# New hand-written orders of the instructions on all engines in a perceiver block (one core)

## What is computed

```python
# part 1: decoder, 4 layers, 16 heads of 16 features
for l in range(4):
    h  = rmsnorm(x, n1[l]);  q, k, v = split(h @ Wqkv[l].T + bqkv[l])
    q, k = rope(q), rope(k)
    x += softmax(q @ k.T / 4 + causal) @ v @ Wo[l].T + bo[l]
    qc = rmsnorm(x, n2[l]) @ Wq_c[l].T
    kc, vc = split(memory @ Wkv_c[l].T)      # keys j with itok-128 < j <= itok
    x += softmax(qc @ kc.T / 4 + lookback) @ vc @ Wo_c[l].T
    h3 = rmsnorm(x, n3[l])
    x += silu(h3 @ Wg[l].T) * (h3 @ Wu[l].T) @ Wd[l].T      # 1024 wide
# part 2: each token attends with sigmoids to its 16 predecessors, then layernorm, gamma, beta
# part 3: gated FFN of width 1024: weights rounded to -1, 0, 1 times mean |w|, activations to 8 bits
```

## Time and profile before

| | us |
|---|---|
| three runs | 622.4, 620.0, 622.28 |
| median | 622.28 |
| the profiled execution | 619.67 |
| its span in the trace | 617.9 |
| mean granted clock of TensorE in it | 0.991 |

### The profile page before, as it was taken

How to read it: one execution, slowest core, us unless ns; L and a number is a source line. 1 busy time by engine, 2 the same in 40 slices (tenths; PEclk the granted TensorE clock), 3 DMA queues, 4 the chain that set the end, 5 groups by cost and what they waited for, 6 DMA issues and landing times.

```text
span 617.9 us, 13676 instructions
## 1 busy us (share of the span) xinstructions
PE 564.1 (91%) x5806; PEld 421.8 (68%) x5806; DVE 353.5 (57%) x680; ACT 279.5 (45%) x490; POOL 117.7 (19%) x124
## 2 busy tenths in 40 slices
PE   4989998999999899999998989999898989999855
PEld 1666655988767566988766658987666558897523
DVE  5896445466564454674554455574554364752787
ACT  0254444633355336433544446342554547445523
POOL 4252100012323100020612000122312001252110
PEclk9999999999999999999999999999999999999969
DMA  8800020010500200201400200204000200000001
GB/s 334 345 2 25 12 69 2 5 65 1 205 2 4 102 1 3 68 1 27 180 1 36 70 2 2 69 1 189 16 2 1 71 0 2 0 1 2 2 1 39
DMA packets 4676, 30.29 MB, mean 49 GB/s; under 512 B 1153, under 2 KB 1665, under 8 KB 2818
## 3 DMA queue, kind: packets, MB, share of 16 engines
q1 hardware_dynamic: 4610, 29.35, 12.5%
HBM read 28.82 MB, written 0.52 MB: 47 GB/s over the span
## 4 chain that ended last, share of the span: by engine, by line
PE 77%; DVE 10%; ACT 8%; issue 3%; POOL 1%; DMA 1%; SPq 0%; DVEq 0%; POOLq 0%
PE psD L326 18%; PE QD L621 12%; PE psD L634 9%; PE QD L408 6%; PE QD L443 4%; ACT PTR L1253 3%; PE psD L320 3%; PE QD L436 3%; PE QD L394 3%; DVE AQ L1803 3%; PE psD L463 2%; PE QD L431 2%; PE psD L359 2%; PE psD L484 2%; PE psD L470 2%
## 5 line engine op out<-in xcount | busy, mean ns | idle before, releaser
L1253 ACT ACTIVATE PTR<-QD 128x2048 f32<-128x2048 f32 x40 | 75.1, 1878 | 41.8 <-PE QD L443 21.5
L326 PE MATMUL psD<-WAB,hT 128*128 128x256 f32 (+1 forms) x216 | 70.1, 465 | 2.2 <-DVE hT L1744 2.2
L2492 POOL TENSOR_TENSOR rstd<-ms,mhalf 128x2 f32<-128x2 f32 x26 | 19.9, 764 | 271.8 <-DVE ms L1729 270.6
L1803 DVE TENSOR_REDUCE AQ<-QD 128x8 f32<-128x2048 f32 (+1 forms) x24 | 55.0, 2290 | 27.0 <-PE QD L408 27.0
L621 PE MATMUL QD<-HH,WFH 128*128 128x256 f32 x224 | 67.4, 301 | 0.4 <-DVE WFL L1903 0.4
L1903 DVE TENSOR_TENSOR WFL<-WC,WFH 128x512 fp32r<-128x512 f32 x64 | 48.0, 755 | 32.2 <-ACT WFH L1297 32.1
L621 PE MATMUL QD<-HL,WFH 128*128 128x256 f32 x224 | 63.3, 283 | 0.0
L621 PE MATMUL QD<-HH,WFL 128*128 128x256 f32 x224 | 63.3, 283 | 0.0
L1800 DVE TENSOR_REDUCE AQ<-QD 128x16 f32<-128x2048 f32 x16 | 36.7, 2293 | 39.9 <-PE QD L408 39.9
L634 PE MATMUL psD<-WC,HID 128*128 128x256 f32 x256 | 58.2, 380 | 0.0
L326 PEld LDWEIGHTS psD<-WAB,hT 128*128 128x128 f32 x216 | 39.7, 195 | 21.0 <-issue 14.2
(11 more groups left out here) (172 smaller groups left out, 1021.2 us busy)
## 6 DMA issues: line engine op xcount, KB each, us to landing
WC<-in_wc SPq DMA_DIRECT2D x4, 3072.0 KB, 10.9
WAB<-in_wa SPq DMA_DIRECT2D x4, 1024.0 KB, 4.9
WAB<-in_wb SPq DMA_DIRECT2D x4, 1024.0 KB, 4.7
WF<-in_wf SPq DMA_DIRECT2D x1, 3072.0 KB, 22.8
bias<-in_bias SPq DMA_DIRECT2D x4, 512.0 KB, 3.4
WAB<-in_wt SPq DMA_DIRECT2D x1, 1024.0 KB, 6.0
X<-in_x SPq DMA_DIRECT2D x2, 256.0 KB, 2.8
out_x<-X SPq DMA_DIRECT2D x4, 128.0 KB, 2.4
```

The source lines that it names most:

```text
L326: mm = pe.matmul(bank(l, use)[:, col:col + n], lhs(k), rhs(k), start=(k == 0), stop=(k == KT - 1))
L1253: nc.scalar.activation(PTR[:, r % 2, :], QD[:, :], ACT.Exp, scale=SCALE).then_inc(t_exp, 1)
L1803: v = dve.tensor_reduce(QKR[b][:, t, 0, h, MAXROW].rearrange("p (s r) -> p r s", r=SG_H), QD[:, :].rearrange("p (r s n) -> p r s n", r=4, ...
```

## The change

On TensorE, ScalarE, VectorE and GpSimd the calls of the helpers stand in another order. The calls are the same in kind and number on each engine; no helper is changed, and SP's queue is not. The cuts between prologue, `layer` and the last layer are put elsewhere: on TensorE `layer(l)` now begins with `down(l - 1, 0, ...)` and ends with `gate_up(l, 0, 7)`; on ScalarE it begins with `exp(l, 6)` and ends with `squares(l + 1, 1, 1)`; on VectorE it ends with `residual(l + 1, 0, "wo0")`; on GpSimd it begins with `causal(l, 3)`. The number of blocks is read, and the branch taken, after `pv(0, 1)` on TensorE (before: after `cross_qT(0, 1, 1)`), after `query_max_strips(0, 1)` on ScalarE, after `sines(0, 1, 1)` on GpSimd, and after `cross_q(0, 0)` on VectorE.

TensorE, one layer (layers 1 to 3; in layer 0 alike in its second half). The first block is the order before, the second the new one, from `values(l, 0)` to `cross_qT(l, 0, 1)`:

```diff
-values(l, 0)            maxima_T(l, 1)          norm_T(l, 0, 1)
-scores(l, 2)            queries_keys(l, 1, 0)   pv(l, 0)
-scores_T(l, 1)          maxima_T(l, 2)          outputs_T(l, 0)
-queries_keys(l, 1, 1)   scores_T(l, 2)          rotated_T(l, 1, 0, 1)
-pv(l, 1)                rotated_T(l, 1, 0, 0)   values(l, 1)
-scores(l, 3)            rotated_T(l, 1, 1, 0)   outputs_T(l, 1)        pv(l, 2)
+values(l, 0)            norm_T(l, 0, 1)
+scores(l, 2)            maxima_T(l, 1)          queries_keys(l, 1, 0)  pv(l, 0)
+scores_T(l, 1)          queries_keys(l, 1, 1)   maxima_T(l, 2)
+rotated_T(l, 1, 0, 1)   rotated_T(l, 1, 0, 0)   scores_T(l, 2)
+outputs_T(l, 0)         pv(l, 1)
+scores(l, 3)            rotated_T(l, 1, 1, 0)   outputs_T(l, 1)        pv(l, 2)
...
 out_proj(l, 0, "wo0", Wo, "oT0")
+maxima_T(l, 4)
 scores(l, 5)
-maxima_T(l, 4)
 cross_kT(l, 0)
-pv(l, 3)
+values(l, 1)
 scores_T(l, 4)
 norm_T(l, 1, 0)
 maxima_T(l, 5)
-outputs_T(l, 3)
+pv(l, 3)
 cross_q(l, 0)
 scores_T(l, 5)
+cross_qT(l, 0, 0)
+outputs_T(l, 3)
 pv(l, 4)
-cross_qT(l, 0, 0)
 cross_qT(l, 0, 1)
```

TensorE, all layers, rounds 8 and 9, and the tail:

```diff
 maxima_T(l, 9)
 norm_T(l, 2, 0)
+pv(l, 8)
 scores_T(l, 9)
-pv(l, 8)
 gate_up(l, 0, 0)
-gate_up(l, 0, 1)
 outputs_T(l, 8)
 pv(l, 9)
+gate_up(l, 0, 1)
+outputs_T(l, 9)
 gate_up(l, 0, 2)
 gate_up(l, 0, 3)
 gate_up(l, 0, 4)
-outputs_T(l, 9)
 gate_up(l, 0, 5)
...
 rounded_T(0)
+window_pv(1, 1)
 quantised_gate_up(0, 0)
+out_proj(NL, 1, "mwo1", Wt[:, 3, :, :], "pw1")
 quantised_gate_up(0, 1)
-window_pv(1, 1)
 quantised_gate_up(1, 0)
-out_proj(NL, 1, "mwo1", Wt[:, 3, :, :], "pw1")
-hidden_T(0)
 quantised_gate_up(1, 1)
 rounded_T(1)
 quantised_gate_up(2, 0)
 quantised_gate_up(2, 1)
+hidden_T(0)
```

ScalarE, last layer (the rounds 1 to 5 of the last layer now stand at the end of `layer`, without sums between them):

```diff
 sum_abs(0)
 sum_abs(1)
 sum_abs(2)
-self_strips(NL - 1, 1, 0, 1)
-strip_outputs(NL - 1, 1)
...
-exp(NL - 1, 3)
 sum_abs(3)
-squares(NL - 1, 1, 0)
...
-exp(NL - 1, 4)
 sum_abs(4)
-exp(NL - 1, 5)
 sum_abs(5)
-query_strips(NL - 1, 0, 0)
...
-squares(NL - 1, 1, 1)
 exp(NL - 1, 6)
 sum_abs(6)
 query_max_strips(NL - 1, 7)
 exp(NL - 1, 7)
 sum_abs(7)
...
 exp(NL - 1, 8)
 sum_abs(8)
 query_max_strips(NL - 1, 9)
+strip_outputs(NL - 1, 8)
 exp(NL - 1, 9)
 sum_abs(9)
 sum_abs(10)
 sum_abs(11)
-strip_outputs(NL - 1, 8)
 split_high(NL - 1, 3)
+strip_outputs(NL - 1, 9)
 silu_table()
```

VectorE, prologue, and its tail:

```diff
 normalise(0, 0, 0)
+small_constants()
+weigh_T(0, 0, 0)
 layernorm_stats(1, 1, X0)
-weigh_T(0, 0, 0)
...
 maxima(0, 0)
+biased_v(0, 0)
+maxima(0, 1)
 biased_qk(0, 1, 0)
 cosines(0, 1, 0)
-maxima(0, 1)
-biased_v(0, 0)
+blocks_to_go()
+maxima(0, 2)
 add_sines(0, 1, 0)
-maxima(0, 2)
 biased_qk(0, 1, 1)
 cosines(0, 1, 1)
-blocks_to_go()
+masks()
+add_sines(0, 1, 1)
 biased_v(0, 1)
-add_sines(0, 1, 1)
-masks()
 divide(0, 0)
...
 quantised_hidden(0, 0)
-quantised_hidden(0, 1)
-hidden_scales(0)
-quantised_hidden(1, 0)
 window_sum(1)
 layernorm_stats(5, 1, X)
 window_gamma(1)
 window_residual(1)
+quantised_hidden(0, 1)
 layernorm_stats(7, 1, X0)
-round_hidden(0)
+hidden_scales(0)
 layernorm_apply(7, 1, X0, hs, done)
+quantised_hidden(1, 0)
...
 round_hidden(3)
+hidden_T(2)
 output(0)
-hidden_T(2)
```

More of the change, by code:

```diff
@@ L835, in layer @@
                 gate_up(l, 0, 7)
[L836 to L878, removed]
             pe.wait_ge(c_ld, 16)
@@ L1000, in rest @@
-                rotated_T(1, 0, 0, 0)
-                gate_up(0, 1, 7)
-                pe.wait_ge(consts_set, 1)
-                scores(1, 0)
-                rotated_T(1, 0, 1, 0)
-                down(0, 1, range(0, 4))
-                scores(1, 1)
-                down(0, 1, range(4, FT))
-                maxima_T(1, 0)
-                rotated_T(1, 0, 1, 1)
-                scores_T(1, 0)
-                values(1, 0)
-                maxima_T(1, 1)
-                norm_T(1, 0, 1)
-                scores(1, 2)
@@ L1031, in rest @@
                     layer(l, further)
+                down(NL - 2, 0, range(0, 4))
+                norm_T(NL - 2, 2, 1)
+                down(NL - 2, 0, range(4, FT))
+                gate_up(NL - 2, 1, 0)
+                gate_up(NL - 2, 1, 1)
+                gate_up(NL - 2, 1, 2)
+                norm_T(NL - 1, 0, 0)
+                gate_up(NL - 2, 1, 3)
+                queries_keys(NL - 1, 0, 0)
+                gate_up(NL - 2, 1, 4)
+                gate_up(NL - 2, 1, 5)
+                queries_keys(NL - 1, 0, 1)
@@ new lines, in rest @@
+                gate_up(NL - 2, 1, 6)
+                rotated_T(NL - 1, 0, 0, 0)
+                rotated_T(NL - 1, 0, 0, 1)
+                gate_up(NL - 2, 1, 7)
+                scores(NL - 1, 0)
+                rotated_T(NL - 1, 0, 1, 0)
+                down(NL - 2, 1, range(0, 4))
+                scores(NL - 1, 1)
+                down(NL - 2, 1, range(4, FT))
+                maxima_T(NL - 1, 0)
+                rotated_T(NL - 1, 0, 1, 1)
+                scores_T(NL - 1, 0)
+                values(NL - 1, 0)
@@ new lines, in rest @@
+                norm_T(NL - 1, 0, 1)
+                scores(NL - 1, 2)
+                maxima_T(NL - 1, 1)
+                queries_keys(NL - 1, 1, 0)
+                pv(NL - 1, 0)
+                scores_T(NL - 1, 1)
+                queries_keys(NL - 1, 1, 1)
+                maxima_T(NL - 1, 2)
+                rotated_T(NL - 1, 1, 0, 1)
+                rotated_T(NL - 1, 1, 0, 0)
+                scores_T(NL - 1, 2)
+                outputs_T(NL - 1, 0)
+                pv(NL - 1, 1)
+                scores(NL - 1, 3)
@@ L2296, in rest @@
                 split_low(0, 10)
+                mean_square(1, 0, 0)
+                hidden(0, 1, 0)
+                normalise(1, 0, 0)
+                split_low(0, 11)
+                split_low(0, 12)
+                weigh_T(1, 0, 0)
+                split_low(0, 13)
+                split_low(0, 14)
+                hidden(0, 1, 1)
+                biased_qk(1, 0, 0)
+                cosines(1, 0, 0)
+                hidden(0, 1, 2)
+                hidden(0, 1, 3)
+                add_sines(1, 0, 0)
@@ new lines, in rest @@
+                hidden(0, 1, 4)
+                hidden(0, 1, 5)
+                biased_qk(1, 0, 1)
+                cosines(1, 0, 1)
+                split_low(0, 15)
+                hidden(0, 1, 6)
+                add_sines(1, 0, 1)
+                hidden(0, 1, 7)
+                maxima(1, 0)
+                maxima(1, 1)
+                residual(0, 1, "y1")
+                mean_square(1, 0, 1)
+                normalise(1, 0, 1)
+                weigh_T(1, 0, 1)
+                biased_v(1, 0)
@@ L2297, in rest @@
+                maxima(1, 2)
+                biased_qk(1, 1, 0)
+                cosines(1, 1, 0)
+                add_sines(1, 1, 0)
+                biased_qk(1, 1, 1)
+                cosines(1, 1, 1)
+                divide(1, 0)
+                add_sines(1, 1, 1)
+                maxima(1, 3)
+                divide(1, 1)
+                divide(1, 2)
+                maxima(1, 4)
+                cross_kv(1, 0)
+                residual(1, 0, "wo0")
                 for l in range(1, NL - 1):
```

771 lines of the change are left out of this document (376 added, 395 removed).

## The result

The changed kernel took **624.07 us** (median of seven runs, 622.99 to 625.11), the kernel before, measured beside it, 621.42 (seven runs, 619.43 to 622.40). The ratio is 1.005 with a 95% interval of 1.0034 to 1.0067: slower by about half a per cent, 2.65 us between the medians. The forecast was 622.7 us, a loss of 0.4 against a median of 622.28 in the first three runs; the measured time lies inside the stated range and inside the forecast case's own range of 620 to 625. The loss is larger than the forecast's, and the last part says why the time is near all the same.

A forecast was written before the change was run, and what follows sets the result against it. TensorE, busy 564.1 of 617.9 us, bounds the kernel; a new order can win only its stops. 2.7 + 2.0 - 2.1 - 2.5 - 0.5 = -0.4, a loss added to the median 622.28: 622.7 us, range 617.0 to 627.5.

The forecast's parts named there:

- forecast case: Whole kernel: gains and losses cancel, 622.7 us, own range 620 to 625, chance 0.44.
- Step 1: Layers 1 to 3: values(l, 1) behind the output projection cuts stops of 2.01 us to 1.1, 2.7 us gained in all.
- Step 2: All four layers: pv(8) ahead of scores_T(9) fills a stop of 0.42 us, 0.5 each, 2.0 us gained.
- what would make it wrong: Signs: slack in ScalarE's block, a new stop in the gate and up products, or unseen waits from rotating four banks.
- Step 3: Last layer, ScalarE: six sum_abs in one block make TensorE stand about 4.8 us ahead of scores_T(7); net loss 2.1 us.
- Step 4: Prologue: VectorE's blocks_to_go ahead of maxima(0, 2) makes a stop of about 4.1 us ahead of scores_T(1); loss 2.5 us.
- Step 5: Tail: VectorE sets the pace and the first product starts some 0.5 us later; loss 0.5 us.
- The rival that had it fall in both: Prologue and last layer: both long stops bring the clock down, 3.1 us each, 628.9 us; chance 0.10.
- point of decision: Last layer's new stop: the clock falls once TensorE stands longer than about 4.2 us; 625.9 us, chance 0.22.

The follow-up runs named there:

- before_values: The kernel before with only values(l, 1) of layers 1 to 3 moved behind cross_kT(l, 0), and what must follow on VectorE and ScalarE: 622.87 us, ratio 1.0042.
- best_split_early: sums_idle with layer 0 up to round 7 in the old order, and split_low(l, 15) ahead of biased_qk and cosines on VectorE: 611.27 us, ratio 0.9851.
- before_sums_block: The kernel before with only sum_abs(0) to (5) moved into one block ahead of exp(NL - 1, 6): 624.24 us, ratio 1.0068.
- block_later: The changed kernel with only VectorE's blocks_to_go moved back to its old place behind cosines(0, 1, 1): 628.30 us, ratio 1.0113.
- sums_two_early: The changed kernel with only sum_abs(0) and (1) moved into ScalarE's idle time, four sums left in the block: 624.35 us, ratio 1.0044.
- sums_idle: The changed kernel with sum_abs(0) to (5) moved to where ScalarE waits for the last layer's first maxima: 618.08 us, ratio 0.9957.

## Why the prediction was right or wrong

**The bound** was right: TensorE's stops and their releasers decided, and every difference found is one of its stops, or of its clock behind one.

**Step 1, values(l, 1).** Forecast 0.9 a layer. In the changed kernel the stops came as told (0.30 ahead of scores_T(4), 0.49 ahead of scores(3)). The step itself was put too simply: alone it wins 0.2 a period and leaves a stop of 1.22 (before_values). The changed kernel also moves the rotated tiles' transposes ahead of scores_T(2), and there the stop is 0.49; that the pair gives the 0.9 is argued from this, no run holds the pair alone. The diff held both; my text priced one.

**Step 2, pv(8).** Forecast 0.5 each, 2.0. The gain is real, 2.5 us, and again belongs to a pair: alone it is nothing, with gate_up(l, 0, 1) behind pv(9) it is there. The last layer's stop was 1.03 instead of 0.42.

Steps 1 and 2 together were to give 1.4 a period, and 0.95 came. The missing 0.4 is the stop of 0.38 ahead of gate_up(l, 1, 7), where split_low(l, 15) stands behind biased_qk and cosines on VectorE (before, cosines came after it). Near it lies a move on TensorE that my account of the change left out: queries_keys(l + 1, 0, 1) stands behind gate_up(l, 1, 5) instead of ahead of gate_up(l, 1, 4); its part in the stop is not shown. My text named such a stop as what would make it wrong, but had not walked VectorE's list there. best_split_early took it away and won 0.63 a period.

**Step 3, the sums.** Size and place of the stop were right (4.70 for 4.8), and the net of 2.1 without the clock fits: between the marks around it 2.66 were lost, and 2.1, the 1.7 of the clock and 0.4 of the new stop in gate_up, less the 1.4 of steps 1 and 2, make 2.8. before_sums_block gives 4.2 less 2.4 of the clock, 1.8, for the sums alone.

**Step 4, the prologue.** The stop was right, 4.06 for 4.1, but most of its reason was not; that the lengths agree is luck. I put it to the block ahead of maxima(0, 2); the block adds 1.55 to a stop of 2.5 that TensorE's own order makes. And the loss was 3.95, not 2.5: 1.7 of it is the clock again.

**Step 5, the tail,** forecast a loss of 0.5, was 0.13 in the two traces. The tail's clock was low for 12.7 us in the changed kernel's trace and 9.2 before, so its 0.13 isn't free of it. No stop stands at the branch itself, but it ties the block to an early place: with the block later, exp(0, 1) waits (block_later).

**The step that failed** is in the forecast case: that the clock stays up in the two new stops. The rival that had it fall in both was right in mechanism and wrong in price. I took half of 8.5 us and less, 3.1 each, from the tail; in the changed kernel's profile it was 1.7 each, since the clock came back after 3.4 us of dense work, though in other kernels' executions it came to up to 3.1. And its point of decision, 4.2 us, doesn't exist as such: the clock fell in or just behind stops of 2.51, 3.20, 4.06 and 4.70 and behind 1.03, and stayed up in one of 3.33. In the changed kernel's own tail it fell at 593.7, 2.2 us after TensorE had last worked.

**Luck.** The time came out near the forecast because errors offset each other. Two falls that the forecast put at nothing cost 3.4 us and the stops in gate_up 1.2; 1.3 came back in the last layer and the tail; and the median that the forecast was added to, 622.28 of three runs, lies 0.9 above the 621.42 of all seven. The loss itself, 2.65, is more than six times the 0.4 that was forecast.

By the marks: the forecast, cut at them, was a loss of 2.5, gains of 1.4 and 1.4, a loss of 0.7 (1.4 won, 2.1 lost), a gain of 0.5 and a loss of 0.5, together -0.4. Measured were -3.95, +0.94, +0.96, -2.66, +1.44 and -0.13, together -3.4. The 3.0 between the sums is 3.4 of the clock, three times 0.4 of the stop in gate_up, and against it about 1.3 that the second half of the last layer and the tail gave beyond the forecast (pv(8) there filled a stop of 1.03, and a stop of 0.44 in gate_up went); the 0.3 that is left lies in the prologue, whose loss without the clock is 2.25 and not 2.5.

**Left open:** why the clock falls in one execution and not in the next (no run held the clock up with the stops in place, so its share rests on the marks and on runs whose stops are gone), and what in the new prologue beyond scores(0, 2) ahead of scores_T(0, 1) is late.

## What to carry to other kernels

Walk each edit of an order together with the step that takes up the freed or lost time: pv(8) alone moved a stop and won nothing, with its partner 2.5 us. Small independent work (sums, counts, casts) belongs where its engine already waits for a long step, never in one block in front of a copy that the busiest engine needs. And a stop of the matmul engine of a few microseconds has two prices: its length, and the slower clock that may follow it, 1.7 to 3.1 us here.

## What the runs showed of the hardware that was not expected

- In or behind a stop the granted clock went to 1.2 GHz for 3.4 us (changed kernel, both places) or 6.8 us (before_sums_block, sums_two_early). One and the same stop of 4.06 us had 3.4 in the changed kernel's execution and 6.8 in that of sums_idle, a cost of 1.7 and 2.8 us. The executions of sums_two_early scatter in two groups (620.3 to 621.2 and 623.7 to 625.7 us); that this is the clock is likely and not shown for each.
- A stop of 3.33 us left the clock alone, while two of 0.82 and 1.03 close together were followed by a fall in the same execution, and not in the kernel before. The Trainium skill (TensorE: Matmul & The Clock Gate, HAM oscillation — how this bites in real kernels) has the clock fall back when the engine idles between bursts. The falls at the stops of 4.06 and 4.70 agree with it; the two others show that the length of a single stop doesn't decide (3.33 against 1.03 in one execution).
- An operation of VectorE on 31 numbers took 1.85 us beside a GpSimd select and 0.16 without it.
